# TensorE's order in a slot: out of the unit three back first, the scores second

## The chip, the cores and the metric

The kernel runs on one core of a Trainium2 chip. The metric is device time in microseconds (us) of one execution. The core has five engines, each with its own instruction stream run in order: TensorE (PE in the profile; PEld is its weight load), VectorE (DVE), ScalarE (ACT), GpSimd (POOL) and SyncE (SP), which here issues the DMAs. They wait for one another by semaphores.

## The reference, cut to what matters

For x of shape (2, 512, 512), with 32 query heads and 8 key/value heads of width 128:

```python
xn = layernorm(x)
q, k, v = xn @ Wq.T, xn @ Wk.T, xn @ Wv.T      # heads split off; q and k then RMS-normed per head
scores = q . k / sqrt(128) + slope[head] * (key - query), masked above the diagonal
attn = softmax(scores)
s = (attn @ v, heads joined) @ Wo.T
g = silu(16 * sum over 8 experts of softmax(xn @ Wr.T + br) * (xn @ A) @ B)    # rank 16 each
y = x + s * g
```

## The kernel before

**Units.** The 1024 rows of x are 8 blocks of 128 (4 of each batch), and the 32 heads are 8 groups of 4 query heads with one key/value head. A unit is one row block of one group: 64 units, u = 8g + block. Because of the causal mask a unit of block t has t mod 4 + 1 key blocks of 128: one, two, three, four, and again.

**Precision.** Nearly each matmul is three: fp32 values are split into a high and a low part (names end in `_hi`, `_lo`), and `three` (lines 1266 to 1268) does hi·hi, hi·lo and lo·hi into the same bank. ScalarE makes the high part by a copy, VectorE or GpSimd the low part by a subtraction.

**One unit's way.** TensorE projects q, k and v of the unit (`project`). ScalarE squares q and k (lines 717, 720), VectorE sums the squares (`square_sums`, line 1007), GpSimd takes the inverse root (lines 541, 545: `inv`), VectorE normalizes k and q (lines 1018, 1023) and turns them by 32x32 blocks (line 1032); DMAs through DRAM finish the turn (`qk_moved`), and ScalarE and VectorE split it into `q_hi`, `k_hi` (lines 700, 707) and `q_lo`, `k_lo` (lines 981, 985). TensorE then does the `scores` of the four heads: three matmuls a head, of 128 columns per key block (a unit with one key block does it in plain fp32, line 1405). VectorE adds the bias and takes the row maximum (`bias`, line 949), ScalarE does the exponentials (line 669), VectorE the reciprocals of their sums (line 956), ScalarE scales (line 677), VectorE turns the probabilities (`square_probs`, line 970), DMAs move them, ScalarE makes `pt_hi` (line 732), GpSimd `pt_lo` (line 551; two blocks of one unit in eight by VectorE, line 1045). TensorE does `mix`, probabilities by v: 3 matmuls of 512 columns for each key block. ScalarE makes `o_hi` of it (line 683), VectorE `o_lo` (`mixed_lo`, line 993). TensorE does `out`, the product with Wo: 12 matmuls of 512 columns, and VectorE adds it to `acc` (line 1064).

**Slots.** All engines run through slots, one for each unit t, and each has its order in a slot written out by hand (`slot`). A slot works on several units at once: the scores of t, the mix of t-2, the out of t-3, and the projection of t+3. On VectorE a slot begins with the biases of t, has the sums of t+2 between them, then k and q of t+2, the add of out(t-3), the turn of t's probabilities with `k_lo`, `q_lo` of t+1 in between, and ends with `o_lo` of t-2. Where t mod 8 is 5 (`W_SLOT`) it has another order: sums and v_lo first, then biases, then two blocks of pt_lo and the splits of the next group's projection weights (line 1038); GpSimd splits the other half (line 524). In slots with t mod 8 = 2 ScalarE and GpSimd also split the next group's Wo (lines 629, 535); `out` of the first unit of a group waits for it head by head.

**The loop.** Slots 3 to 10 stand in a hardware loop over 7 groups, and 3 to 5 behind it; slot 2 and the closing part (`end`) are written beside it.

**The waits at a slot's start on TensorE.** `scores(t)` waits for `k_lo` and `q_lo` of t (from VectorE's slot t-1) and for the biases of t-1, which free its banks; the fourth head of a long unit waits for the first bias of t. `out(t-3)` waits for `o_lo` of t-3, which ends VectorE's slot t-1, and for the add of out(t-4).

Of the kernel before, what the change touches and what calls it, by code (L numbers as in the profile page):

```python
# [132 lines left out]
def build(nc, x, wqkv, wo, aw, bt, br, qkw, consts, y):  # L133
    with ExitStack() as ctx:
# [210 lines left out]
        def here(t, left):  # L345

            return 0 <= t < BLOCKS * left
# [915 lines left out]
        def _(pe):  # L1263
            def three(out, a_hi, a_lo, b_hi, b_lo, start, stop):

                pe.matmul(out, a_hi, b_hi, start=start, stop=False)  # L1266
                pe.matmul(out, a_hi, b_lo, start=False, stop=False)  # L1267
                return pe.matmul(out, a_lo, b_hi, start=False, stop=stop)  # L1268
# [39 lines left out]
            def project(g, t, chunks=range(KC)):  # L1308

                if two_banks(t) and t % BLOCKS > 0:  # L1310
                    for c in chunks:
                        project_q(g, t, c)
                    for c in chunks:
                        project_kv(g, t, c)
                elif two_banks(t):
                    for c in range(EARLY_W):
                        project_q(g, t, c)
                    for c in range(EARLY_W):
                        project_kv(g, t, c)
                    for c in range(EARLY_W, KC):  # L1320
                        project_q(g, t, c)
                        project_kv(g, t, c)
                else:
                    for c in chunks:
                        project_q(g, t, c)
                        project_kv(g, t, c)
# [58 lines left out]
            def scores(g, t, h):  # L1385

                n, hs, b = keys_of(t) * P, slice(h * HD, (h + 1) * HD), t // QB % BATCH
                if h == 0:
                    pe.wait_ge(qk_lo_ready, K_AND_Q_LO(g, t + 1, 0))
                    if t % QB == 0:  # L1390
                        pe.wait_ge(k_full_ready, PER_BATCH(g, t, 1))

                if t < 2:
                    if t > 0 or h >= 2:
                        pe.wait_ge(biased_ready, PER_HEAD(g, t, h - 1))
                    if h == 0:
                        pe.wait_ge(lt_lo_done, t + 1)

                elif h == 0:
                    pe.wait_ge(biased_ready, PER_HEAD(g, t, 0))  # L1400
                elif h == 3 and not has_half(t):
                    pe.wait_ge(biased_ready, PER_HEAD(g, t, 1))
                out = score_bank(t, h)
                if t % QB == 0:
                    last = pe.matmul(out, q_full[:, hs], k_full[:, :], start=True, stop=True)
                else:
                    last = three(out, q_hi[:, hs], q_lo[:, hs], k_hi[:, b, 0:n], k_lo[:, b, 0:n], True, True)
                last.then_inc(scores_ready, 1)
# [26 lines left out]
            def mix(g, u, left):  # L1435

                i, b = u % QB, u // QB % BATCH
                pe.wait_ge(v_lo_ready, ONE(g, u, 1))
                if u > 0:
                    pe.wait_ge(o_lo_ready, ONE(g, u - 1, 1))  # L1440
                for j in range(i + 1):
                    if by_pe(u, left):
                        pe.wait_ge(pt_lo_by_dve, last_turns(u) + j + 1)
                    elif by_both(u) and j >= BY_POOL:
                        pe.wait_ge(moved_lo_by_dve, DVE_BLOCKS(g, u, j - BY_POOL + 1))
                    else:
                        pe.wait_ge(pt_lo_by_pool, POOL_BLOCKS(g, u, j + 1))
                    last = three(mix_ps[:, :], v_hi[:, b, j, :], v_lo[:, b, j, :], pt_hi[:, j, :], pt_lo[:, j, :], j == 0, j == i)
                last.then_inc(mix_ready, 1)

            def out(g, u):

                pe.wait_ge(o_lo_ready, ONE(g, u, 1))
                pe.wait_ge(acc_ready, 1 + ONE(g, u - 1, 1))
                for h in range(HPG):
                    if u % BLOCKS == 0:
                        pe.wait_ge(wo_lo_done, (g + u // BLOCKS) * HPG + (h + 1))
                    last = three(out_ps[:, :], o_hi[:, h, :], o_lo[:, h, :], wo_hi[:, h, :], wo_lo[:, h, :], h == 0, h == HPG - 1)
                last.then_inc(out_ready, 1)
# [25 lines left out]

            def slot(g, t, left):

                if here(t, left):
                    for h in range(HPG):
                        scores(g, t, h)  # L1490
                if here(t - 3, left):
                    out(g, t - 3)
                if here(t - 2, left):
                    mix(g, t - 2, left)
                if here(t + 3, left):
                    project(g, t + 3)
# [78 lines left out]
            for c in range(KC):  # L1575
                project_kv(0, 4, c)
            slot(0, 2, GROUPS)
            pipeline(pe, slot)
            end(GROUPS - 1)

# [32 lines left out]
```

## Time and profile before

| | us |
|---|---|
| median of 3 runs (lowest, highest) | 762.62 (760.61, 764.43) |
| the profiled execution | 757.6 |
| its span, from the first to the last instruction | 755.8 |
| TensorE busy (matmul) | 718.8, 95% |
| VectorE busy | 602.9, 80% |
| ScalarE busy | 561.8, 74% |
| GpSimd busy | 364.3, 48% |
| mean granted clock of TensorE, of full speed | 0.996 |

Busy times are of instructions; matmul records overlap, since a matmul's end is drawn after the next one's start. In a timeline a row has the start and the duration in us, the engine, the line, the operation, the tile written, "<-", the tiles read, the shape, and in brackets the idle time of the engine ahead of it and what ended it. In a table of windows a row has the stretch, its length, the busy time of PE, PEld, DVE, ACT and POOL with the number of instructions in brackets behind each, the granted clock of TensorE, the share of the DMA engines and GB/s. A row of waits has the instruction that waited, the one that ended the wait, the total in us, the number of times and the longest.

### The profile page before, as it was taken

Reading aid. Unit: us, or ns where it says so; the run is one execution under the profiler, and the core shown is the slowest. Engines: PE = TensorE matmul, PEld = TensorE weight load, DVE = VectorE, ACT = ScalarE, POOL = GpSimd, SP = SyncE. Lnnn points to the kernel's source line nnn. Section 1 sums busy time; section 2 is a strip of 40 time slices with the busy share of each in tenths; the row PEclk is TensorE's granted clock in tenths of the full one; section 3 lists DMA queues with packets and bytes.
Section 4 is the critical chain, followed back from the end, with each engine's and each line's share of the span. In section 5 each row is a group of like instructions: output and inputs, shape, how many; then the busy total and the mean of one; then the engine's idle time right before and its main releaser. Section 6 shows DMA issues by size and latency. Waiting matters only on the chain.

```text
span 755.8 us, 14611 instructions
## 1 busy us (share of the span) xinstructions
PE 718.8 (95%) x3736; PEld 608.6 (81%) x3736; DVE 602.9 (80%) x1468; ACT 561.8 (74%) x1440; POOL 364.3 (48%) x343
## 2 busy tenths in 40 slices
PE   7897999999999999999999999999999999999785
PEld 7786888878888788888888788887888788887665
DVE  7857798778978898678987789697987789788764
ACT  4566787696787788686877878776876967778662
POOL 4224354454544653554534743644544544446256
PEclk9999999999999999999999999999999999999999
DMA  8015969578686868787695777768685786867642
GB/s 298 1 29 143 299 154 255 164 221 241 168 273 152 239 185 245 198 225 228 163 283 144 220 214 222 228 167 268 162 250 167 221 236 176 265 153 196 195 134 83
DMA packets 215877, 148.68 MB, mean 197 GB/s; under 512 B 49072, under 2 KB 206640, under 8 KB 215728
## 3 DMA queue, kind: packets, MB, share of 16 engines
q1 hardware_dynamic: 215856, 148.43, 69.5%
q8 instruction: 9, 0.15, 0.1%
q14 instruction: 12, 0.10, 0.1%
HBM read 86.17 MB, written 62.19 MB: 196 GB/s over the span
## 4 chain that ended last, share of the span: by engine, by line
PE 56%; issue 13%; DVE 12%; POOL 8%; ACT 4%; SPq 3%; DMA 3%; POOLq 0%; DVEq 0%; ACTq 0%
PE qkv_ps L1266 6%; PE qkv_ps L1267 6%; PE qkv_ps L1268 6%; PE out_ps L1266 5%; PE out_ps L1268 5%; PE out_ps L1267 5%; PE score_ps L1266 4%; PE score_ps L1268 3%; PE score_ps L1267 3%; PE mix_ps L1266 3%; PE mix_ps L1268 3%; PE mix_ps L1267 3%; POOL w_lo L524 2%; PE turn_ps L1266 2%; SPq L449 2%
## 5 line engine op out<-in xcount | busy, mean ns | idle before, releaser
L551 POOL TENSOR_TENSOR pt_lo<-x_sb,pt_hi 128x512 fp32r<-128x512 f32 x137 | 174.3, 1298 | 240.6 <-ACT pt_hi L732 240.5
L669 ACT ACTIVATE probs<-probs,neg_max 128x128 f32<-128x128 f32 (+3 forms) x256 | 141.8, 556 | 62.0 <-DVE neg_max L949 61.6
L949 DVE CUSTOM_DVE_ANT_0 probs<-score_ps,cst,slope 128x128 f32<-128x128 f32 (+3 forms) x256 | 129.5, 546 | 34.0 <-PE score_ps L1268 25.6
L677 ACT ACTIVATE probs<-probs,recip 128x128 f32<-128x128 f32 (+3 forms) x252 | 126.3, 549 | 8.5 <-DVE recip L956 8.5
L1266 PE MATMUL qkv_ps<-w_hi,xt_hi 128*128 128x256 f32 (+1 forms) x392 | 126.0, 321 | 2.7 <-DVE xt_lo L892 1.4
L1267 PE MATMUL qkv_ps<-w_lo,xt_hi 128*128 128x256 f32 (+1 forms) x392 | 125.7, 321 | 0.0
L1268 PE MATMUL qkv_ps<-w_hi,xt_lo 128*128 128x256 f32 (+1 forms) x392 | 125.2, 319 | 0.0
L541 POOL TENSOR_TENSOR inv_rms<-sums,minus_half 128x5 f32<-128x5 f32 x64 | 78.8, 1231 | 78.6 <-DVE sums L1007 78.4
L1266 PE MATMUL out_ps<-wo_hi,o_hi 128*128 128x512 f32 x252 | 101.9, 404 | 3.3 <-DVE o_lo L993 3.3
L970 DVE STREAM_TRANSPOSE squared<-probs 128x256 f32<-128x256 f32 (+3 forms) x124 | 101.8, 823 | 2.0 <-ACT probs L677 1.1
L1267 PE MATMUL out_ps<-wo_lo,o_hi 128*128 128x512 f32 x252 | 100.2, 398 | 0.0
L1268 PE MATMUL out_ps<-wo_hi,o_lo 128*128 128x512 f32 x252 | 100.1, 397 | 0.0
L732 ACT ACTIVATE pt_hi<-x_sb 128x512 fp32r<-128x512 f32 x153 | 86.2, 623 | 8.1 <-DMA x_sb<-turning 8.1
L1266 PEld LDWEIGHTS qkv_ps<-w_hi,xt_hi 128*128 128x128 f32 x392 | 74.3, 190 | 12.2 <-DVE xt_lo L892 1.7
L1267 PEld LDWEIGHTS qkv_ps<-w_lo,xt_hi 128*128 128x128 f32 x392 | 74.3, 190 | 8.6
L1266 PE MATMUL score_ps<-k_hi,q_hi 128*128 128x256 f32 (+2 forms) x192 | 67.9, 354 | 11.9 <-DVE k_lo L985 7.0
L1268 PEld LDWEIGHTS qkv_ps<-w_hi,xt_lo 128*128 128x128 f32 x392 | 74.3, 190 | 5.7
L700 ACT ACTIVATE q_hi<-qk_moved 128x512 fp32r<-128x512 f32 x46 | 28.9, 628 | 49.1 <-DMA qk_moved<-turning_qk 48.7
L1268 PE MATMUL score_ps<-k_hi,q_lo 128*128 128x256 f32 (+2 forms) x192 | 64.8, 337 | 0.0
L1267 PE MATMUL score_ps<-k_lo,q_hi 128*128 128x256 f32 (+2 forms) x192 | 64.6, 337 | 0.0
L1266 PE MATMUL mix_ps<-pt_hi,v_hi 128*128 128x512 f32 (+1 forms) x160 | 62.3, 389 | 0.0
L1018 DVE TENSOR_TENSOR squares<-qkv_ps,inv 128x128 f32<-128x128 f32 x64 | 18.4, 288 | 54.9 <-POOL inv L545 54.8
(172 smaller groups left out, 1637.5 us busy)
## 6 DMA issues: line engine op xcount, KB each, us to landing
turning_qk<-qk_squared SPq DMA_DIRECT2D x244, 80.0 KB, 1.9
qk_moved<-turning_qk SPq DMA_DIRECT2D x61, 320.0 KB, 3.4
turning<-squared SPq DMA_DIRECT2D x120, 128.0 KB, 2.4
x_sb<-turning SPq DMA_DIRECT2D x30, 512.0 KB, 5.1
w_raw<-wqkv SPq DMA_DIRECT2D x32, 384.0 KB, 5.5
turning<-squared SPq DMA_DIRECT2D x120, 96.0 KB, 2.0
x_sb<-turning SPq DMA_DIRECT2D x30, 384.0 KB, 4.2
turning<-squared SPq DMA_DIRECT2D x128, 64.0 KB, 1.8
```

What stands on the lines that cost most here:

```text
L541: nc.gpsimd.tensor_tensor(inv_rms[:, :], sums[:, :], minus_half[:, 0:NORMED], ALU.pow).then_inc(inv_rms_ready, 1)
L551: nc.gpsimd.tensor_tensor(by_quad(pt_lo, j), moved_block(t, j), by_quad(pt_hi, j).bitcast(F32), ALU.subtract).then_inc(pt_lo_by_pool, 1)
L669: nc.scalar.activation(probs[:, h, 0:n], probs[:, h, 0:n], ACT.Exp, bias=neg_max[:, h:h + 1], scale=-1.0, accum_out=total[:, h:h + 1]).the ...
L677: nc.scalar.activation(to[:, h, 0:n], probs[:, h, 0:n], ACT.Copy, scale=recip[:, h:h + 1]).then_inc(probs_ready, 1)
L700: nc.scalar.activation((q_hi[:, :] if ui > 0 else q_full).rearrange("p (h a n) -> p h a n", h=HPG, a=QUADS), q_turned, ACT.Copy).then_inc( ...
L732: nc.scalar.activation(by_quad(pt_hi, j), moved_block(t, j), ACT.Copy).then_inc(pt_hi_ready, 1)
L949: nc.vector.tensor_tensor_reduce(probs[:, h, 0:n], score_bank(t, h), cst[:, C_DIST + SEQ - n:C_DIST + SEQ], slope[:, h:h + 1], HUGE, ALU.a ...
L970: nc.vector.transpose(blocks[:, :, 0:keys_of(t), :, :], probs[:, h:h + 2, 0:n].rearrange("p h (j k n) -> p h j k n", k=QUADS, n=QUAD)).the ...
L1018: nc.vector.tensor_tensor(qk_norm[:, HPG, :], k_ps, inv[:, HPG:NORMED].broadcast_to([P, HD]), ALU.mult).then_inc(k_norm_ready, 1)
L1266: pe.matmul(out, a_hi, b_hi, start=start, stop=False)
L1267: pe.matmul(out, a_hi, b_lo, start=False, stop=False)
L1268: return pe.matmul(out, a_lo, b_hi, start=False, stop=stop)
```

## The change

In TensorE's `slot` the two parts `scores(g, t, h)` for the four heads and `out(g, t - 3)` change places. `mix` and `project` stay third and fourth. The closing part and all other engines keep their orders.

```diff
             def slot(g, t, left):
 
+                if here(t - 3, left):
+                    out(g, t - 3)
                 if here(t, left):
                     for h in range(HPG):
                         scores(g, t, h)
-                if here(t - 3, left):
-                    out(g, t - 3)
                 if here(t - 2, left):
                     mix(g, t - 2, left)
                 if here(t + 3, left):
```

## Rows read from the trace of the kernel before

**Rows 1.** The page, part 1: busy us (share of the span) and instructions of each engine.
```profile
PE 718.8 (95%) x3736; PEld 608.6 (81%) x3736; DVE 602.9 (80%) x1468; ACT 561.8 (74%) x1440; POOL 364.3 (48%) x343
```

**Rows 2.** Timeline of VectorE around a one-key slot (4 mod 8): start, duration.
```profile
344.78 0.65 DVE L993 TENSOR_TENSOR o_lo<-mix_ps,o_hi 128x512 fp32r<-128x512 f32 x1
...
348.26 0.29 DVE L1018 TENSOR_TENSOR squares<-qkv_ps,inv 128x128 f32<-128x128 f32 x1 [0.74 <-POOL inv L545]
...
351.80 0.69 DVE L981 TENSOR_TENSOR q_lo<-qk_moved,q_hi 128x512 fp32r<-128x512 f32 x1 [0.79 <-ACT q_hi L700]
```

**Rows 3.** Windows from first bias to end of o_lo, eight slots; one turn; seven turns.
```profile
345.36:353.85 8.49, 8.37 (x39) 6.97 (x40) 6.92 (x22) 4.73 (x16) 2.07 (x3) 1.00 0.95 272
356.07:367.16 11.09, 10.77 (x55) 9.03 (x54) 11.09 (x25) 10.55 (x26) 9.32 (x7) 1.00 0.56 137
367.28:376.48 9.20, 9.20 (x49) 7.82 (x47) 8.88 (x21) 7.61 (x19) 2.64 (x4) 1.00 0.71 183
377.34:387.29 9.95, 9.95 (x50) 8.30 (x50) 9.53 (x21) 8.61 (x19) 2.63 (x4) 1.00 0.90 263
388.19:396.17 7.98, 7.98 (x38) 6.58 (x38) 6.66 (x21) 4.34 (x16) 3.35 (x4) 1.00 0.97 301
398.44:409.47 11.03, 11.03 (x58) 9.49 (x57) 8.46 (x22) 7.79 (x23) 6.52 (x7) 1.00 0.45 108
409.42:420.08 10.66, 10.66 (x55) 9.03 (x54) 9.01 (x22) 8.85 (x21) 4.05 (x5) 1.00 0.75 192
420.16:432.46 12.30, 10.91 (x55) 8.68 (x54) 9.64 (x21) 10.48 (x26) 9.29 (x9) 1.00 0.77 224
345.36:432.38 87.02, 85.27 (x436) 72.16 (x436) 71.11 (x173) 67.76 (x174) 43.00 (x41) 1.00 0.75 211
73.94:681.12 607.18, 596.42 (x3053) 505.00 (x3052) 498.82 (x1206) 474.14 (x1219) 298.21 (x279) 1.00 0.76 212
```

**Rows 4.** Timeline of TensorE where out waited for o_lo: out's and mix's first matmul.
```profile
345.49 0.50 PE L1266 MATMUL out_ps<-wo_hi,o_hi 128*128 128x512 f32 x1 [0.41 <-DVE o_lo L993]
...
348.39 0.40 PE L1266 MATMUL mix_ps<-pt_hi,v_hi 128*128 128x512 f32 x1
```

**Rows 5.** Timeline of TensorE: first score matmul of four slots.
```profile
366.36 0.34 PE L1266 MATMUL score_ps<-k_hi,q_hi 128*128 128x384 f32 x1
...
376.25 0.39 PE L1266 MATMUL score_ps<-k_hi,q_hi 128*128 128x512 f32 x1
...
387.35 1.06 PE L1405 MATMUL score_ps<-k_full,x_sb 128*128 128x128 f32 x8
...
397.28 0.28 PE L1266 MATMUL score_ps<-k_hi,q_hi 128*128 128x256 f32 x1
```

**Rows 6.** Waits, in total: two of VectorE's.
```profile
DVE squares L1018 <- POOL inv L545: 54.8, 46, 2.6
...
DVE q_lo L981 <- ACT q_hi L700: 15.7, 13, 3.5
```

**Rows 7.** Timelines of ScalarE, GpSimd and VectorE in slot 2 mod 8.
```profile
414.86 0.63 ACT L700 ACTIVATE q_hi<-qk_moved 128x512 fp32r<-128x512 f32 x1 [0.65 <-DMA qk_moved<-turning_qk]
...
417.39 5.06 POOL L535 TENSOR_TENSOR wo_lo<-wo_raw,wo_hi 128x512 fp32r<-128x512 f32 x4 [4.55 <-ACT wo_hi L629]
...
419.39 0.69 DVE L993 TENSOR_TENSOR o_lo<-mix_ps,o_hi 128x512 fp32r<-128x512 f32 x1 [1.35 <-ACT o_hi L683]
```

**Rows 8.** Windows on TensorE's clock: three waits, behind the second, and around it.
```profile
68.81:72.25 3.44, 0.00 (x1) 0.01 (x1) 0.95 (x2) 1.75 (x4) 0.00 (x0) 1.00 1.05 317
712.28:715.08 2.80, 0.00 (x1) 0.01 (x1) 2.80 (x7) 1.80 (x5) 0.95 (x1) 1.00 0.56 130
716.00:719.00 3.00, 3.00 (x8) 2.35 (x8) 1.41 (x6) 1.67 (x6) 0.00 (x0) 0.50 0.51 125
710.00:720.00 10.00, 6.76 (x24) 5.60 (x25) 6.96 (x21) 5.38 (x14) 1.27 (x1) 0.83 0.52 137
720.90:723.23 2.33, 0.00 (x1) 0.01 (x1) 1.01 (x3) 1.68 (x4) 0.00 (x0) 1.00 0.93 286
```

## The prediction

> **What bounds the kernel now.** I read the page's busy shares first: TensorE is busy 95% of the span, VectorE 80% [rows 1]. A kernel read no further looks TensorE-bound, and then two parts of one engine's order could change places free of charge. So I went to the order of the slots. Slot t of VectorE begins with the biases of unit t (line 949), which need the scores of t, and ends with o_lo of unit t-2 (line 993), which in the next slot the out product needs. The table of windows over one turn of eight slots, each cut from the first bias to the end of o_lo, gives TensorE 85.27 us busy of 87.02, and VectorE 71.11 [rows 3]. The eight VectorE runs together last 80.70 us; so VectorE has 6.3 us per eight slots (0.8 a slot) between its last and its next first instruction, and the rest of its idle time lies inside the runs. Behind four of the eight runs the next bias follows o_lo within 0.12 us (one o_lo ends at 344.78 + 0.65 = 345.43, and the next run is already cut at 345.36; records overlap by some 0.07) [rows 2, 3]. That is possible only because the scores of t are done while VectorE still works on unit t-1: they need k_lo and q_lo, which VectorE writes before its last transpose and o_lo. TensorE is the bound, but VectorE is close behind, through a gap that the scores fill early.
>
> **The change, part by part.** Nothing is added or removed: the same 12 out matmuls, the same scores, on 59 slots (t = 3 to 61; in slot 2 there is no unit three back, and the closing part writes its own order). What moves is the wait: out(t-3) waits for o_lo of t-3, the last instruction of VectorE's slot t-1, and now the scores of t stand behind that wait, on an engine whose instructions run in order. VectorE's next instruction (in seven kinds of slot of eight a bias) waits for those scores. This closes a loop: VectorE's run, then out, then the first scores, then VectorE's run.
>
> The part of the loop on TensorE. Where out waited for o_lo, its first matmul started 0.06 us after o_lo's end (345.43 to 345.49), and the first mix matmul behind the twelve at 348.39: 2.90 us [rows 2, 4]. From the first score matmul to the first bias it took 0.92 us with three key blocks (366.36 to 367.28), 1.09 with four (376.25 to 377.34), 0.84 with one (387.35 to 388.19) and 1.16 with two (397.28 to 398.44), where the first bias wants two heads [rows 3, 5]. So the gap on VectorE is 2.96 plus that: 3.88, 4.05, 3.80, 4.12. Each kind occurs twice in eight slots: 31.7 us.
>
> The part on VectorE: its runs, less the stalls that the gap now hides. Runs of rows 3, in order of the slots t mod 8 = 4, 5, 6, 7, 0, 1, 2, 3:
> - 4 (8.49): 0.79 of it is the wait for q_hi, behind a DMA [rows 2, 6]. The DMA is issued from the slot before and gains 3.8 us: 7.70.
> - 5, 6, 7: as they are, 11.09, 9.20, 9.95. In slot 5 VectorE does sums and v_lo ahead of the biases, so these fall into the gap, and the run from the first bias is unchanged.
> - 0 (7.98, 1.32 idle) and 1 (11.03, 2.57 idle): nearly all of it waits for inv from GpSimd [rows 3, 6], which is late behind its pt_lo of the slot before. With a longer slot GpSimd has done that, and what is left is the chain sums to inv itself, 0.74 at the slot 4 where GpSimd was free [rows 2]. I leave 0.74 in each: 7.40 and 9.20.
> - 2 (10.66): o_lo waits 1.35 for o_hi, since ScalarE splits wo in between; ScalarE itself lost 0.65 at q_hi to a DMA, which goes [rows 7]: 10.01.
> - 3 (12.30, 2.66 idle): GpSimd is behind its four wo_lo, 5.06 us [rows 3, 7]; that wait goes, since two biases of four key blocks cover the chain (the other four-key slot, 7, has 0.42 idle in all): 9.64.
>
> Sum 74.2; with the gaps 105.9 per eight slots. Before, seven turns took 607.18 us [rows 3], 86.7 each. The difference, 19.2, is 2.40 a slot, and for 59 slots 141 us. On the profiled execution of 757.6 us (span 755.8): 899. Bounds of this sum: if every stall in the runs went, the runs are VectorE's busy time, 70.2, and the time 869; if none went, 80.7, and 947.
>
> What the moved order could also meet: in slot 3 the first unit of a new group takes wo_lo, whose four parts GpSimd ends at about 417.39 + 5.06 = 422.45, 2.4 us after o_lo's end at 420.08; out's last head starts 2.2 us after it, so 0.2 us, eight times [rows 7]: nothing, but up to now the scores covered it. The projection and mix still come behind both scores and out, so what they wait for (k_norm and v_lo of the slot, GpSimd's pt_lo) stands worse against them by 2.9 us at most. K_norm starts 2.9 us after the first bias in the slot of [rows 2], while mix and the query part of the projection still keep TensorE busy behind the scores; I cost it at nothing, and where it shows, it delays TensorE inside a slot in which TensorE would only wait for o_lo at the end.
>
> **TensorE's clock.** TensorE's work is 85.27/8 = 10.7 us a slot; a slot will last 11.2 (one key block) to 15.2 (slot 5), so it will wait for o_lo in nearly all, and 2.4 us or more in six kinds of eight, some 44 slots. The trace has three waits of about that length, 3.44, 2.80 and 2.33 us, in which TensorE did nothing; after the second the granted clock fell to 0.50, that is from 2.4 to 1.2 GHz, and after the others it did not [rows 8]. The stretch of ten microseconds that holds the fall has 0.83 on average [rows 8]: 3.4 us at half speed, 1.7 lost. One wait in three falling makes 15 falls. What runs then is out and the scores, the part on the loop; some of a stretch may lie past it, so 1.6 each: 24 us. Bounds: none, 0; every one of the 44, 75.
> The Trainium skill (TensorE: Matmul & The Clock Gate, "HAM oscillation — how this bites in real kernels") describes kernels whose matmul groups are parted by waits and fall back to half clock at each of them; by that rule the time would be that of rival 2. The trace agrees at one wait of three.
>
> So 757.6 + 141 + 24 = 923 on the profiled execution's footing. The median of the three runs, 762.6, is 0.7% above that execution; I do not scale for it, and 923 is the forecast.
>
> **Rivals.**
> 1. The loop as above, and the clock stays at its upper level: 899. For it: two waits of three, one of 3.44 us, passed without a fall [rows 8]. Against: 44 waits offer many occasions.
> 2. The clock falls at nearly every long wait: 899 + 75 = 974. For it: the fall after 2.80 us. Against: the wait of 3.44 us without one [rows 8].
> 3. The runs shrink to VectorE's busy time, as GpSimd, ScalarE and the DMAs catch up in the gap: 869 without any fall of the clock, some 880 with a few. Against: the 0.74 from sums to inv, and ScalarE's wo split, lie inside the run.
> 4. Not slower. VectorE is idle 20% of the span [rows 1], about 2.0 us a slot, and if the out product (2.9 us) ran while VectorE finished something else, the idle time would take most of it: 762. It would decide if a run and its gap together fitted into today's 607.18/56 = 10.84 us a slot [rows 3]. The shortest does not: 7.40 + 3.80 = 11.2; even with runs at VectorE's busy time the mean is 8.8 + 4.0 = 12.7.
>
> **How the numbers follow.** The forecast (loop and some falls, 905 to 945): 55 in 100. Rival 1: 17. Rival 2: 10. Rival 3: 10. Rival 4: 2; the other 6 are sizes that I have wrong in either direction, past these cases. The range is 875 to 970: it takes in rivals 1 and most of 3 and 2, and the two bounds of the stalls. Slower by over 0.5% (a difference smaller than that can't be told from none here) 0.97, within 0.5% 0.02, faster 0.01.
>
> **What would show it.** Right: VectorE's biases wait for the scores in all 59 slots, 3.8 to 4.1 us each at full clock, some 230 us in sum; out waits for o_lo in nearly all, and TensorE's busy share falls to about 80%; the waits of VectorE for inv drop to at most 0.74 each; a turn lasts 106 us or more. The granted clock over the loop tells the clock's term: 24 us lost is a mean of about 0.97. Wrong: biases that start right after o_lo as now, a bias gap well under 3.8, or inv waits as long as before.

## The result, and the profile after

The changed kernel takes 960.62 us (median of 4 runs, 952.76 to 962.63) against 762.71 before: ratio 1.258, 95% interval 1.254 to 1.261. The profiled execution took 960.04, its span 958.2. The range of the prediction (875 to 970) holds it; the forecast, 923, is 38 us short. Ratios go by the fast executions of both kernels: one that lies over 1.5% above the fastest of its kernel is left out (here one, of the kernel with half the fillers).

The page's busy line of the changed kernel, to be held against [rows 1]:

```profile
PE 789.9 (82%) x3736; PEld 652.7 (68%) x3736; DVE 610.5 (64%) x1468; ACT 556.9 (58%) x1440; POOL 362.7 (38%) x343
```

VectorE, ScalarE and GpSimd do the same work in nearly the same busy time, over a span 202 us longer. TensorE alone has more, 71 us, with the same number of instructions: matmuls that ran slower.

The table of windows of the changed kernel, cut as in [rows 3]: eight slots (t = 20 to 27) from the first bias to the end of o_lo, then one turn, then seven turns.

```profile
321.47:328.91 7.44, 6.41 (x35) 5.34 (x33) 6.66 (x22) 5.82 (x20) 1.36 (x2) 1.00 1.00 321
333.02:343.50 10.48, 8.46 (x40) 6.05 (x38) 10.48 (x24) 7.23 (x20) 4.93 (x3) 1.00 0.43 105
347.36:356.56 9.20, 6.35 (x35) 5.37 (x33) 8.88 (x21) 7.78 (x20) 2.86 (x4) 1.00 0.49 131
362.14:372.10 9.96, 7.38 (x39) 6.11 (x37) 9.53 (x21) 8.62 (x19) 2.23 (x3) 0.97 0.52 155
378.69:387.15 8.46, 6.45 (x35) 5.38 (x34) 7.68 (x21) 7.12 (x22) 4.20 (x4) 1.00 0.51 165
392.81:402.09 9.28, 7.35 (x40) 6.16 (x38) 8.77 (x21) 6.53 (x19) 2.64 (x3) 1.00 0.25 58
407.52:417.74 10.22, 6.34 (x35) 5.36 (x33) 9.91 (x21) 9.06 (x22) 4.37 (x5) 0.91 0.33 80
424.10:434.01 9.91, 7.34 (x38) 6.00 (x36) 9.42 (x20) 8.56 (x20) 2.24 (x3) 1.00 0.41 125
321.47:437.85 116.38, 97.02 (x439) 79.75 (x438) 72.33 (x173) 67.08 (x174) 42.80 (x40) 0.90 0.57 158
80.26:877.95 797.69, 663.14 (x3053) 545.49 (x3052) 505.33 (x1204) 469.76 (x1218) 298.95 (x280) 0.92 0.58 161
```

All runs but one (8.46, before 7.98) are as short as before or shorter: in this turn 74.95 us together, where [rows 3] has 80.70. All that was lost lies between a run's end and the next run's start: 328.91 to 333.02 is 4.11, 372.10 to 378.69 is 6.59. Seven turns went from 607.18 to 797.69 us, so 190.5 of the 202 us are there.

The timeline of VectorE, first biases of five slots (in brackets the idle time ahead):

```profile
321.47 0.35 DVE L949 CUSTOM_DVE_ANT_0 probs<-score_ps,cst,slope 128x128 f32<-128x128 f32 x1 [3.84 <-PE score_ps L1405]
333.02 0.48 DVE L949 CUSTOM_DVE_ANT_0 probs<-score_ps,cst,slope 128x256 f32<-128x256 f32 x1 [3.19 <-PE score_ps L1268]
347.36 0.62 DVE L949 CUSTOM_DVE_ANT_0 probs<-score_ps,cst,slope 128x384 f32<-128x384 f32 x1 [3.79 <-PE score_ps L1268]
362.14 0.75 DVE L949 CUSTOM_DVE_ANT_0 probs<-score_ps,cst,slope 128x512 f32<-128x512 f32 x1 [5.58 <-PE score_ps L1268]
378.69 0.35 DVE L949 CUSTOM_DVE_ANT_0 probs<-score_ps,cst,slope 128x128 f32<-128x128 f32 x1 [6.59 <-PE score_ps L1405]
```

Two sorts of gap are seen: about 3.8 us (4.1 with two key blocks), and 5.6 to 6.6. (The second row shows 3.19 because sums and v_lo come ahead of the biases in that slot.) The timeline of TensorE ahead of the bias at 362.14 shows why:

```profile
356.62 0.50 PE L1266 MATMUL out_ps<-wo_hi,o_hi 128*128 128x512 f32 x1 [2.90 <-DVE o_lo L993]
...
357.41 0.40 PE L1266 MATMUL out_ps<-wo_hi,o_hi 128*128 128x512 f32 x1
...
358.35 0.63 PE L1266 MATMUL out_ps<-wo_hi,o_hi 128*128 128x512 f32 x1
...
359.63 0.63 PE L1266 MATMUL out_ps<-wo_hi,o_hi 128*128 128x512 f32 x1
...
360.91 0.54 PE L1266 MATMUL score_ps<-k_hi,q_hi 128*128 128x512 f32 x1
```

TensorE waited 2.90 us for o_lo and began out; a microsecond later its matmuls take 0.63 us in place of 0.40, and out ends 4.29 us after its start, not 2.90. Two windows from the same place, for the granted clock (the third number from the end):

```profile
356.00:359.00 3.00, 2.38 (x8) 1.93 (x9) 0.56 (x1) 0.30 (x2) 1.57 (x2) 0.80 0.82 202
359.50:361.50 2.00, 2.00 (x6) 1.55 (x6) 0.00 (x0) 0.00 (x0) 0.00 (x0) 0.57 0.86 219
```

While TensorE does out at half clock, VectorE, ScalarE and GpSimd do nothing at all (0.00 in the second row): the loop in one line. The waits, in total:

```profile
DVE probs L949 <- PE score_ps L1268: 211.6, 47, 6.6
PE out_ps L1266 <- DVE o_lo L993: 136.6, 60, 6.3
...
DVE probs L949 <- PE score_ps L1405: 70.7, 16, 6.6
...
DVE squares L1018 <- POOL inv L545: 19.4, 39, 1.0
```

Before, VectorE's waits for scores were these; its wait for inv was 54.8 [rows 6].

```profile
DVE probs L949 <- PE score_ps L1268: 25.6, 19, 2.3
...
DVE probs L949 <- PE score_ps L1405: 7.1, 9, 0.9
```

### The profile page after: what moved, and what is told of

It reads as the page before. It is cut to its first block, busy times and chain, and to the rows that moved or that the text cites. A ratio compares the mean times of both kernels' runs of the same rounds, so it can differ in the third digit from the quotient of the medians.

```text
span 958.2 us, 14611 instructions
## 1 busy us (share of the span) xinstructions
PE 789.9 (82%) x3736; PEld 652.7 (68%) x3736; DVE 610.5 (64%) x1468; ACT 556.9 (58%) x1440; POOL 362.7 (38%) x343
## 4 chain that ended last, share of the span: by engine, by line
issue 34%; DVE 23%; PE 20%; POOL 12%; ACT 5%; DMA 3%; SPq 2%; DVEq 1%; POOLq 0%; ACTq 0%
POOL pt_lo L551 6%; PE out_ps L1266 6%; PE out_ps L1267 5%; PE out_ps L1268 4%; POOL inv_rms L541 4%; DVE squared L970 3%; DVE k_lo L985 3%; DVE o_lo L993 3%; ACT probs L677 2%; DVE q_lo L981 2%; DVE squares L1023 2%; DVE probs L949 2%; DVE sums L1007 2%; SPq L449 2%; DVE acc L1064 1%
## 5 line engine op out<-in xcount | busy, mean ns | idle before, releaser
L1266 PE MATMUL out_ps<-wo_hi,o_hi 128*128 128x512 f32 x252 | 127.1, 504 | 136.6 <-DVE o_lo L993 136.6
L541 POOL TENSOR_TENSOR inv_rms<-sums,minus_half 128x5 f32<-128x5 f32 x64 | 74.9, 1171 | 276.2 <-DVE sums L1007 276.2
L1266 PEld LDWEIGHTS out_ps<-wo_hi,o_hi 128*128 128x128 f32 x252 | 58.5, 232 | 160.6 <-DVE o_lo L993 117.0
L1267 PE MATMUL out_ps<-wo_lo,o_hi 128*128 128x512 f32 x252 | 120.2, 477 | 0.0
L1268 PE MATMUL out_ps<-wo_hi,o_lo 128*128 128x512 f32 x252 | 120.0, 476 | 0.0
L1268 PEld LDWEIGHTS out_ps<-wo_hi,o_lo 128*128 128x128 f32 x252 | 60.2, 239 | 15.8
L1267 PEld LDWEIGHTS out_ps<-wo_lo,o_hi 128*128 128x128 f32 x252 | 59.9, 238 | 12.2
L1266 PE MATMUL mix_ps<-pt_hi,v_hi 128*128 128x512 f32 (+1 forms) x160 | 64.6, 404 | 4.4 <-DVE pt_lo L1045 4.4
```

The source lines that it names most:

```text
L541: nc.gpsimd.tensor_tensor(inv_rms[:, :], sums[:, :], minus_half[:, 0:NORMED], ALU.pow).then_inc(inv_rms_ready, 1)
```

## The experiments

Two theories stood against each other behind the number. The loop theory: o_lo, the whole of out, the first scores and VectorE's run follow one another, plus a term for the clock that falls in TensorE's waits. Its rivals: that the early wait is the cost, however much work stands behind it; and that the clock alone is. In the code shown, "..." marks lines left out; the kernels with fillers have one line more at the top, so their line numbers are one higher.

**Fillers (clock).** At the end of a TensorE slot, matmuls of no use into the bank of out, as many as leave about 0.5 us of the wait; the next out overwrites them.

```diff
+FILL = (7, 6, 15, 9, 2, 0, 10, 9)
...
                 if here(t + 3, left):
                     project(g, t + 3)
+                if t > 2 and FILL[t % BLOCKS]:
+                    pe.wait_ge(acc_ready, 1 + ONE(g, t - 3, 1))
+                    for _ in range(FILL[t % BLOCKS]):
+                        pe.matmul(out_ps[:, :], xt_hi[:, 0, 0:P], xt_hi[:, 0, 0:SEQ], start=True, stop=True)
```

> Filler matmuls into the idle out bank at the end of each TensorE slot, sized to leave some 0.5 us of each wait for o_lo; their results are overwritten by the next out. Loop theory with a clock term: the granted clock stays at 1.00 over the loop, the 30 long gaps on VectorE (5.4 to 6.6 us) go back to 3.8 to 4.1, and the 55 us by which the gaps exceeded these go: 905 us (895 to 915). Rival, that the long gaps have another cause than the clock (Wo's split, contention): the gaps stay and the time is 950 to 965. Rival, that the falls are the main loss and the loop only their occasion: 765 to 800.

Measured: 910.5 us (908.5 to 910.9), ratio 1.194 (1.189 to 1.199). Its window over the loop and two of its biases:

```profile
80.00:862.00 782.00, 737.02 (x3610) 601.01 (x3608) 530.13 (x1264) 492.07 (x1276) 309.99 (x291) 1.00 0.62 172
```

```profile
350.29 0.75 DVE L950 CUSTOM_DVE_ANT_0 probs<-score_ps,cst,slope 128x512 f32<-128x512 f32 x1 [4.04 <-PE score_ps L1269]
...
364.06 0.35 DVE L950 CUSTOM_DVE_ANT_0 probs<-score_ps,cst,slope 128x128 f32<-128x128 f32 x1 [3.80 <-PE score_ps L1406]
```

The same two slots that had 5.58 and 6.59 have 4.04 and 3.80, with more work on TensorE, not less; of all 59 gaps one is still long (6.42, ahead of the first slot of the loop). The clock cost the changed kernel 960.6 - 910.5 = 50 us, and what is left without it is 148. Both rivals of this expectation fall: the long gaps went with the clock, and 148 us stay when it is up. Whether the 148 are the price of out or of the wait itself is settled by the runs with half of out and with the wait alone, below.

**Half as many fillers.** `FILL = (4, 3, 8, 5, 1, 0, 5, 5)`, all else the same.

> As the run with fillers, with about half of them: the waits for o_lo on TensorE that are left are some 1.2 to 1.8 us, 2.2 in slots with t mod 8 = 3. If the clock falls by the length of the wait, these are shorter than any wait behind which it fell in the changed kernel (1.98 us the shortest), but for slot 3: some 7 falls, 910 to 925. Rival, that it is the share of TensorE's idle time over the loop that lowers the clock: falls in about half of the long-gap slots, 930 to 940.

Measured: 919.2 us (910.2 to 925.5), ratio 1.200 (1.193 to 1.206). In the profiled execution 10 of the 59 gaps were long, where 7 were expected, so the time is as the length of the waits had it; but the rule as I put it is wrong. The falls were not only in slots 3 (5 of 8 there): behind four waits of 1.76 or 1.77 us ahead of a slot 7 the clock fell as well (and behind one of 2.37 ahead of a slot 4, in the last turn), while behind the other three waits there, 1.74 to 1.76 us, and behind three of 2.2 it did not. One of the four, from the timeline of TensorE, and the bias behind it:

```profile
451.96 0.50 PE L1267 MATMUL out_ps<-wo_hi,o_hi 128*128 128x512 f32 x1 [1.77 <-DVE o_lo L994]
```

```profile
457.50 0.75 DVE L950 CUSTOM_DVE_ANT_0 probs<-score_ps,cst,slope 128x512 f32<-128x512 f32 x1 [5.59 <-PE score_ps L1269]
```

What decides between two equal waits, these runs don't settle.

**Half of out ahead.** The changed order, with heads 0 and 1 of out ahead of the scores, 2 and 3 behind them (not shown: `out` takes the heads as a parameter).

```diff
                 if here(t - 3, left):
-                    out(g, t - 3)
+                    out(g, t - 3, range(0, 2))
                 if here(t, left):
                     for h in range(HPG):
                         scores(g, t, h)
+                if here(t - 3, left):
+                    out(g, t - 3, range(2, HPG))
```

> Changed order, but only the first two of out's four heads go ahead of the scores and the other two behind them. Loop theory: the gap on VectorE shrinks by 1.45 us a slot to 2.35 to 2.7 at full clock, a turn of eight slots takes 75 + 20 = 95 us, the time is 825 to 830 plus 0 to 25 for fewer falls of the clock, 840. Rival, that the wait for o_lo ahead of the scores costs, whatever stands behind it: 940 to 965.

Measured: 827.9 us (826.0 to 835.0), ratio 1.088 (1.081 to 1.095). The gap ahead of two first biases, of four and of one key block:

```profile
415.04 0.75 DVE L949 CUSTOM_DVE_ANT_0 probs<-score_ps,cst,slope 128x512 f32<-128x512 f32 x1 [2.64 <-PE score_ps L1268]
...
427.40 0.35 DVE L949 CUSTOM_DVE_ANT_0 probs<-score_ps,cst,slope 128x128 f32<-128x128 f32 x1 [2.40 <-PE score_ps L1405]
```

4.04 became 2.64, 3.80 became 2.40: 1.40 us less, the length of the half of out that moved away. The rival (940 to 965) falls: the wait stands where it stood, and 83 us are gone against the run with fillers.

**The wait alone.** The order of before, and the wait ahead of the scores.

```diff
+                if here(t - 3, left):
+                    pe.wait_ge(o_lo_ready, ONE(g, t - 3, 1))
                 if here(t, left):
                     for h in range(HPG):
                         scores(g, t, h)
                 if here(t - 3, left):
                     out(g, t - 3)
```

> Order of before, with the wait for o_lo of t-3 put ahead of the scores as well (scores, then out behind it). Loop theory: the gap on VectorE is 0.06 us and the head of the scores, about 1.1; run and gap together are 10.4 to 11.2 a slot, near TensorE's own 10.7: 762 to 785 us. Rival, that the early wait is the cost: 900 or more. The wait leaves TensorE idle for 1 us or less at a time, so no falls of the clock in the loop are expected by either.

Measured: 784.5 us (782.8 to 785.4), ratio 1.029 (1.024 to 1.033), at the upper end of what the loop theory allowed. The rival (900 or more) falls: the early wait by itself costs 22 us of the 198. The gap is mostly 1.2 to 1.5 us in six kinds of slot, where 1.1 was expected, and 2.1 to 2.9 in slots 1 and 5: in slot 1 TensorE is still at the projection of the slot before when o_lo ends (502.31), and its first score matmul starts at 503.78, without a wait. With slots this short GpSimd is late as well, and VectorE waits 38.1 us in all for inv.

```profile
501.66 0.65 DVE L993 TENSOR_TENSOR o_lo<-mix_ps,o_hi 128x512 fp32r<-128x512 f32 x1
504.94 0.48 DVE L949 CUSTOM_DVE_ANT_0 probs<-score_ps,cst,slope 128x256 f32<-128x256 f32 x1 [2.63 <-PE score_ps L1268]
```

```profile
DVE squares L1018 <- POOL inv L545: 38.1, 46, 2.4
...
PE score_ps L1266 <- DVE o_lo L993: 28.3, 29, 6.5
```

So a measured series stands, by what is put between o_lo and the scores: nothing 784.5, half of out 827.9 (five gaps in slots with t mod 8 = 3 still long), all of it 910.5 at full clock. A slot of 59 grows by 0.74 us for the first 1.4 us and by 1.40 for the second. The first half is cheaper for two reasons that the traces show. The gaps ahead of slots 1 and 5 hardly grow with it, since they were long already: the one of slot 1 is 2.82 with half of out where it was 2.63 with nothing.

```profile
533.91 0.48 DVE L949 CUSTOM_DVE_ANT_0 probs<-score_ps,cst,slope 128x256 f32<-128x256 f32 x1 [2.82 <-PE score_ps L1268]
```

And as long as the slots are short, GpSimd's lateness is what VectorE would wait for anyway (inv waits of 38.1 us with nothing, 21.5 with half, 19.4 with all of out ahead).

**o_lo early.** The changed order on TensorE; on ScalarE `mixed_hi` goes ahead of the split of q and k, and on VectorE `mixed_lo` right behind `add_out`, so that out may run beside VectorE's turns (shown: VectorE's common slot; slot 5 and ScalarE are changed alike).

```diff
                 if here(t - 3, left):
                     add_out(g, t - 3)
+                if here(t - 2, left):
+                    mixed_lo(g, t - 2, left)
                 if here(t, left):
                     square_probs(g, t, 0)
                 if here(t + 1, left):
                     turned_qk_lo(g, t + 1)
                 if here(t, left):
                     square_probs(g, t, 2)
-                if here(t - 2, left):
-                    mixed_lo(g, t - 2, left)
```

> Changed order on TensorE; on ScalarE o_hi and on VectorE o_lo of t-2 go ahead of the turns of t's probabilities and of k_lo, q_lo of t+1, so that out can run beside these (1.6 to 2.7 us a slot). Loop theory: the gap on VectorE behind its run shrinks to 1.3 to 2.2 us, a turn takes 75 + 14 = 89 us, the time is 778, 770 to 800. Rival, that out ahead of the scores costs its 2.9 us wherever o_lo is made: 900 to 960.

Measured: 820.9 us (818.4 to 825.2), ratio 1.079 (1.073 to 1.085). The direction is the loop theory's, 140 us below the changed kernel, and the rival (900 to 960) falls; but 770 to 800 was missed. The gap is 0.4 to 1.3 us ahead of three kinds of slot (7, 0, 4), 2.1 to 3.5 ahead of four, and 4.7 to 5.6 ahead of slot 3; 1.3 to 2.2 was expected. Out of a group's first unit now waits for Wo's split on GpSimd, from the timeline of TensorE and the waits:

```profile
447.80 0.50 PE L1266 MATMUL out_ps<-wo_hi,o_hi 128*128 128x512 f32 x1 [2.91 <-POOL wo_lo L535]
```

```profile
DVE squares L1018 <- POOL inv L545: 35.3, 40, 2.4
...
PE out_ps L1266 <- POOL wo_lo L535: 22.5, 14, 3.0
```

To tell whether that wait made the miss, the same kernel with the scores first in the slots with t mod 8 = 3:

```diff
+                first = t % BLOCKS != 3
-                if here(t - 3, left):
+                if first and here(t - 3, left):
                     out(g, t - 3)
                 if here(t, left):
                     for h in range(HPG):
                         scores(g, t, h)
+                if not first and here(t - 3, left):
+                    out(g, t - 3)
```

> Kernel of the run with o_hi and o_lo early, but in slots with t mod 8 = 3 TensorE does the scores first as before. In that run out waited there up to 2.9 us for wo_lo from GpSimd, and the clock fell behind it. Theory that this is what kept the run above its 778: VectorE's gap there goes from 4.7 to 5.6 us to 1 or less, 4 us a turn and the clock's falls in the loop go: 785 to 795. Rival, that out ahead of the scores keeps costing its 2.9 us in every slot whatever is done about o_lo: 815 to 825.

Measured: 815.1 us (810.7 to 821.0), ratio 1.070 (1.065 to 1.075): the expectation (785 to 795) failed. The clock goes on falling (0.971 over this profiled execution, 0.980 over that of the run before). The wait for wo_lo is gone, but ahead of the scores of slot 3 TensorE waits as long for k_lo, which VectorE now makes after o_lo:

```profile
452.15 0.49 PE L1266 MATMUL score_ps<-k_hi,q_hi 128*128 128x512 f32 x1 [3.16 <-DVE k_lo L985]
```

So the wait for wo_lo alone was not the cause: behind it stood a second wait of the same length. Nor does the rival hold, though the time lies at the edge of its range (815 to 825): VectorE's gaps behind its run are 0.4 to 3.5 us in this kernel, not 3.8 to 4.1 in every slot. What all of the 815 consists of I did not settle.

**o_lo early in the order of before.** The last kernel's changes on ScalarE and VectorE, TensorE as before.

> Order of before on TensorE (scores first), with o_hi and o_lo early on ScalarE and VectorE. TensorE idles only 1.75 us of 87 in a turn there, so by the theory that it is the bound 755 to 768, no difference that can be told. Rival: the earlier o_lo takes VectorE's time ahead of k_lo, which the scores need, and these now come late: 775 or more.

Measured: 773.6 us (771.8 to 776.0), ratio 1.015 (1.013 to 1.018): 12 us longer, between the theory's range (755 to 768) and the rival's (775 or more). The rival's reason is seen: TensorE's waits for k_lo ahead of the scores of longer units went from 7.0 to 18.5 us (first row before, second row here).

```profile
PE score_ps L1266 <- DVE k_lo L985: 7.0, 4, 3.4
```

```profile
PE score_ps L1266 <- DVE k_lo L985: 18.5, 21, 4.7
```

VectorE's waits for inv rose as well, from 54.8 to 61.1 us, so the share of each in the 12 us is not separated.

No version tried here beats the kernel before.

## Why the prediction was right, and which term was mis-sized

**The loop: right.** The waits stand where they were forecast, VectorE for the scores and TensorE for o_lo, in nearly all of the 59 slots.

**The gap: right to hundredths.** Forecast 3.80, 4.12, 3.88 and 4.05 us for one to four key blocks; measured at full clock 3.84 and 4.11 (321.47 and 333.02 against the run ahead), 3.86 (347.36 - 343.50), and 4.04 with fillers (350.29). The rows of before held the price, since out had waited for o_lo there too [rows 4, 5].

**The runs: right.** Forecast 74.2 us a turn with the stalls that the gap hides taken out, measured 74.95. Waits for inv fell to 0.75 at most in the loop (19.4 us in all). Slots 5 (10.48 for 11.09) and 4 (7.44 for 7.70) came out shorter than said, slots 0 (8.46 for 7.40), 3 (9.91 for 9.64) and 2 (10.22 for 10.01) longer, so that the sum agrees better than its parts; in so far it is luck. Added up over the 59 slots of the profiled execution: runs 551.7 us, gaps 289.1, of which 234 are what gaps of their kinds take at full clock (59 times 3.96; forecast the same) and 55.2 what the clock added.

**The clock: the term mis-sized.** Forecast: one long wait in three lowers it, 15 falls at 1.6 us, 24 us. Measured: 30 of the 59 gaps were long, by 1.84 us each, 55 us, and the fillers took 50 us away. The mean granted clock over the seven turns is 0.92, where 0.97 was named as the sign of 24 us. Two things were off. The number: I took the share, one in three, from three waits of before [rows 8], and it was two in three, 30 falls behind 44 waits of 1.98 us and more. That there are 44 such waits was right, though two of the six kinds are shorter than the 2.4 us forecast (ahead of the slots 7, 0, 1, 2, 3, 4: some 2.9, 2.6, 2.1, 2.0, 4.0, 2.6 us). Length is not all: the clock fell behind all nine waits over 3 us, but ahead of slot 1 (2.06 us) behind 6 of 7 and ahead of slot 4 (2.62) behind 1 of 7. The size: nine of the gaps are over 6.2 us, as at 378.69, where out and the scores' head all ran slow and lost 2.8 us. The Trainium skill (TensorE: Matmul & The Clock Gate, "HAM oscillation — how this bites in real kernels") tells of a kernel that falls back at each of its waits, which are some 3 to 5 us long there. The trace agrees at the nine waits over 3 us, though not at the one of 3.44 us before [rows 8]; of the 35 between 1.98 and 2.93 us, to which the prediction stretched the rule, 21 had a fall.

**The 38 us that the forecast is short.** Against the medians, 26 are the clock's (50 by the fillers, for 24), 7 are the loop's (148 for 141, of which the runs, 74.95 a turn for 74.2, make 5.5), and 5 are the footing: the sum stood on the profiled execution of before, 757.6 us, and the median is 5 us above. The time lies past the case that the prediction thought likeliest (905 to 945); the range holds it because it was drawn wide enough for most of rival 2.

**Rivals.** The clock at its upper level (899) is what the fillers made, 910. Rival 2 (974) came nearest in number, 13 us off; a fall at nearly every long wait is not what happened, but 30 in 44, and 55 us in place of its 75. Runs shrunk to VectorE's busy time (869): the 0.74 and ScalarE's Wo split remained, as said against it. Not slower (762): no run and gap fitted in 10.84 us; the shortest slot took 11.55. Wo's split, costed at nothing with 0.2 us named, shows with fillers: the gap of slot 3 is 4.2 us there, 0.15 more than that of the other four-key slot.

## What to carry to other kernels

An engine 95% busy can still be the cheapest place to lose time: look at what the next engine's first instruction waits for, and which product is made last ahead of it. Work that needs a slot's last product is put behind the work that starts the next slot elsewhere; what stands in between is paid in each round once run and gap no longer fit in a slot. When a forecast opens waits on TensorE in every round, let the range reach from no fall of the clock to one at each of them rather than take a share from a few seen before (here it was 30 of 44, and 10 of 59 with half the fillers), and test it with filler matmuls, which take the clock's part away and leave the loop's.

## What the runs showed of the hardware

Adding work made the kernel faster: the fillers give TensorE up to 15 matmuls more a slot, and 960.6 us became 910.5; the granted clock of the profiled execution went from 0.924 to 0.987.

A small VectorE subtraction that starts while GpSimd makes pt_lo or wo_lo takes up to four times as long. In the changed kernel k_lo of the slot at 378.69 took 1.36 us, while GpSimd made pt_lo from 384.31 on; the same instruction in the turn with the bias at 492.31 took 0.34. First VectorE's two rows, then GpSimd's:

```profile
384.86 1.36 DVE L985 SCALAR_TENSOR_TENSOR k_lo<-qk_moved,both_w,k_hi 128x128 fp32r<-128x128 f32 x1
...
498.49 0.34 DVE L985 SCALAR_TENSOR_TENSOR k_lo<-qk_moved,both_w,k_hi 128x128 fp32r<-128x128 f32 x1
```

```profile
384.31 5.53 POOL L551 TENSOR_TENSOR pt_lo<-x_sb,pt_hi 128x512 fp32r<-128x512 f32 x4 [2.73 <-ACT pt_hi L732]
```

It is this 1.02 us that makes slot 0's run 8.46 where 7.40 was forecast, in six of its seven rounds. Over all nine traces of this case, 131 of the k_lo instructions start while a pt_lo or wo_lo of GpSimd is under way (or at most 0.04 us ahead of one), and every one of them ends 0.14 to 0.16 us after it (in the rows above, the first of the four pt_lo ends at 386.08, k_lo at 386.22); the other 418 take 0.31 to 0.35 us. It doesn't meet every VectorE instruction: 238 o_lo instructions, which read mix_ps, start beside the same GpSimd work and take 0.64 to 0.69 us as always. One such k_lo is what TensorE waits for at 452.15 in the kernel with the scores first in slots 3:

```profile
450.66 1.35 DVE L985 SCALAR_TENSOR_TENSOR k_lo<-qk_moved,both_w,k_hi 128x128 fp32r<-128x128 f32 x1
```

No run here moves GpSimd's work alone, so that GpSimd is what holds k_lo up is read from how regularly the two ends agree, not tested.
